# A recurrent layer in 2048 dependent steps: the output sum on GpSimd, y in two halves, and store addresses named earlier

## The reference, cut to what matters

```python
x = x + _L0_cond_ref(x, cond, W1, b1, W2, b2)   # per channel: x * (2 + gate), see below
x = x + _L1_cond_ref(cond, x, W_z, U_z, C_z, b_z, W_r, U_r, C_r, b_r, W, U, C, b)

def step(h, xs):                                # 2048 times, one after the other
    xzt, xrt, xht = xs
    z = sigmoid(xzt + h @ U_z + vz)
    r = sigmoid(xrt + h @ U_r + vr)
    hh = tanh(xht + r * h @ U + vh)
    h_new = (1.0 - z) * h + z * hh
    return (h_new, h_new)
```

## Time and profile before

| what | value |
|---|---|
| median of 3 runs | 6809.69 us (6809.19 to 6810.33) |
| the profiled execution, its own time | 6811.76 us |
| its span, first to last instruction | 6809.9 us |
| granted TensorE clock, mean | 0.996 |
| busy: PE, PEld, DVE, ACT, POOL | 88%, 83%, 73%, 49%, 0% |
| chain that ended last | PE 71%, DVE 26%, issue 3% |

### The profile page before, as it was taken

The page is one execution under the profiler, slowest core; times in us unless marked ns, Lnnn a source line. Parts: engine busy times, 40 slices in busy tenths (PEclk is TensorE's granted clock), DMA queues, the critical chain, the costliest instruction groups (busy, mean ns, idle before and its releaser), DMA issues.

```text
span 6809.9 us, 488240 instructions
## 1 busy us (share of the span) xinstructions
PE 5998.4 (88%) x200232; PEld 5642.2 (83%) x200232; DVE 4955.6 (73%) x43503; ACT 3331.6 (49%) x22603; POOL 3.5 (0%) x13
## 2 busy tenths in 40 slices
PE   7888888888888888888888888888888888888888
PEld 7888888888888888888888888888888888888888
DVE  5777777777777777777777777777777777777777
ACT  3444444444444444444444444444444444444444
POOL 0000000000000000000000000000000000000000
PEclk8999999999999999999999999999999999999999
DMA  2000000000000000000000000000000000000000
GB/s 84 17 18 15 18 17 18 17 17 17 18 17 18 15 18 17 18 18 15 18 17 18 17 18 15 18 17 18 17 17 17 18 17 18 15 18 18 17 18 15
DMA packets 80315, 129.97 MB, mean 19 GB/s; under 512 B 12336, under 2 KB 18480, under 8 KB 80304
## 3 DMA queue, kind: packets, MB, share of 16 engines
q1 hardware_dynamic: 80304, 129.81, 5.5%
HBM read 20.46 MB, written 8.65 MB: 4 GB/s over the span
## 4 chain that ended last, share of the span: by engine, by line
PE 71%; DVE 26%; issue 3%; SPq 0%; DMA 0%; ACT 0%; ACTq 0%; DVEq 0%
PE pair_r L252 30%; PE ps_z L252 24%; PE pair_h L252 17%; DVE pair_h L487 8%; DVE h_part L522 5%; DVE h_part L541 4%; DVE h_part L527 2%; DVE keep L523 2%; DVE zn L536 2%; DVE h_part L532 2%; PE ps_z L212 0%; DMA u_raw<-in_L_cond_U 0%; PE ps_o L212 0%; DVE u_max L424 0%; PE ps_x L224 0%
## 5 line engine op out<-in xcount | busy, mean ns | idle before, releaser
L252 PEld LDWEIGHTS pair_r<-h_part,u_part 128*128 128x128 f16 x65536 | 1845.1, 96 | 1119.9 <-DVE h_part L541 1115.8
L252 PE MATMUL pair_r<-h_part,u_part 128*128 128x32 f16 x65536 | 2048.7, 177 | 771.1 <-DVE h_part L541 758.6
L252 PE MATMUL pair_h<-rh_part,u_part 128*128 128x32 f16 x65536 | 2016.6, 177 | 12.5 <-DVE rh_part L505 12.5
L252 PE MATMUL ps_z<-h_part,u_part 128*128 128x32 f16 x65536 | 1961.5, 176 | 0.0
L252 PEld LDWEIGHTS pair_h<-rh_part,u_part 128*128 128x128 f16 x65536 | 1842.8, 96 | 17.3 <-DVE rh_part L505 15.7
L252 PEld LDWEIGHTS ps_z<-h_part,u_part 128*128 128x128 f16 x65536 | 1795.3, 95 | 0.0
L487 DVE TENSOR_REDUCE pair_r<-pair_r 128x4 f32<-128x20 f32 x4096 | 759.4, 186 | 818.1 <-PE pair_r L252 615.1
L351 ACT ACTIVATE pair_r<-pair_r 128x4 f32<-128x4 f32 x4096 | 644.8, 158 | 1445.1 <-DVE pair_r L487 1182.4
L487 DVE TENSOR_REDUCE pair_h<-pair_h 128x4 f32<-128x12 f32 x4096 | 717.7, 175 | 665.7 <-PE pair_h L252 665.7
L351 ACT ACTIVATE th_z<-ps_z 128x8 f32<-128x8 f32 x2048 | 364.1, 178 | 1046.0 <-DVE ps_z L487 1046.0
L337 ACT ACTIVATE pair_h<-xp 128x8 f32 (+1 forms) x2049 | 369.9, 181 | 807.8 <-DVE zn L536 807.8
(11 more groups left out here) (70 smaller groups left out, 3275.9 us busy)
## 6 DMA issues: line engine op xcount, KB each, us to landing
w_stage<-w_in SPq DMA_DIRECT2D x384, 256.0 KB, 2.3
x_tok<-in_x SPq DMA_DIRECT2D x68, 128.0 KB, 2.6
out_dram<-o_tok SPq DMA_DIRECT2D x66, 128.0 KB, 2.3
mlp_w<-in_L_cond_W SPq DMA_DIRECT2D x2, 1024.0 KB, 6.9
u_raw<-in_L_cond_U_r SPq DMA_DIRECT2D x1, 1024.0 KB, 5.6
u_raw<-in_L_cond_U_z SPq DMA_DIRECT2D x1, 1024.0 KB, 7.6
u_raw<-in_L_cond_U SPq DMA_DIRECT2D x1, 1024.0 KB, 10.3
w_in<-in_L_cond_W_r SPq DMA_DIRECT2D x4, 256.0 KB, 9.8
```

What stands on the lines that cost most here:

```text
L252: last = nc.tensor.matmul(bank[:, SLOT * m:SLOT * m + WIDE].rearrange("p (r n) -> p r n", n=n), u_part[:, g, part, k, gm * P:(gm + 1) * P] ...
```

## The change

Three edits.

1. `make_out` moves from VectorE to GpSimd. GpSimd gets a loop over the 32 blocks: it waits for s_z_th of the block's first step (the hist copy of the last token stands ahead of that tanh on ScalarE) and adds hist and y_cur with one `tensor_tensor`. It can't scale in the same instruction, so ScalarE's copy into hist is scaled by 1 / H_SCALE. The last output waits for s_copied on GpSimd.
2. `make_y` becomes two instructions of 128x256: the first behind step 2 of the turn, the second, which raises s_y_ok, behind step 3.
3. `store_projection` takes its semaphore count and two offsets, written as three `dve.snap` expressions behind step u = 0 of the round, and indexes flattened views of xp and v_bias with them, behind step u = 3 as before.

```diff
--- before.py
+++ after.py
@@ -185,6 +185,18 @@
             pool.wait_ge(s["umax_ok"], G)
             nc.gpsimd.partition_all_reduce(u_all[:, :], u_max[:, :], P, RMAX).then_inc(s["uall_ok"], 1)
 
+            def make_out(ring):
+                nc.gpsimd.tensor_tensor(oT[:, :, :], hist[:, bass.ds(ring, TB), :].rearrange("p t c -> p c t"),
+                                        y_cur[:, :, :], ALU.add).then_inc(s["o_sum"], 1)
+
+            with pool.Fori(0, NB) as n:
+
+
+                pool.wait_ge(s["z_th"], pool.snap(n * TB + 1))
+                make_out(pool.snap(((n + 1) % 2) * TB))
+            pool.wait_ge(s["copied"], 1)
+            make_out((NB - 1) % 2 * TB)
+
         @block.tensor
         def _(pe):
             pe.wait_ge(s["ident_ok"], 1)
@@ -360,7 +372,7 @@
                     for hf in range(2):
                         tanh(ps_r[hf][:, TANH:TANH + HS], ps_r[hf], R, HS, f"r{hf}_sum", t1, f"r{hf}_th")
 
-                    A(hist[:, prv, :], h_cur[:, :], ACT.Copy)
+                    A(hist[:, prv, :], h_cur[:, :], ACT.Copy, scale=1.0 / H_SCALE)
                     tanh(th_z[:, :], ps_z, Z, S, "z_sum", t1, "z_th")
 
                     seed(pair_r, R, nxt)
@@ -388,7 +400,7 @@
                 with act.Fori(0, GM) as i:
                     steps(act.snap(n * TB + i * BODY + TURN), BODY, act.snap((n % 2) * TB + i * BODY + TURN))
             act.wait_ge(s["h_ok"], T)
-            A(hist[:, (T - 1) % (2 * TB), :], h_cur[:, :], ACT.Copy).then_inc(s["copied"], 1)
+            A(hist[:, (T - 1) % (2 * TB), :], h_cur[:, :], ACT.Copy, scale=1.0 / H_SCALE).then_inc(s["copied"], 1)
             put_out(NB + 1)
 
         @block.vector
@@ -449,13 +461,16 @@
             mlp_layer(1)
             dve.wait_ge(s["gate_ok"], 1)
 
-            def make_y(nb):
-
-                dve.wait_ge(s["x_tr"], nb)
-                V.tensor_tensor(y_next[:, :, :], ps_x[:, :].rearrange("p (c t) -> p c t", t=TB),
-                                gate2[:, :].unsqueeze(2).broadcast_to([P, S, TB]), ALU.mult).then_inc(s["y_ok"], 1)
-
-            make_y(1)
+            def make_y(nb, part):
+                if part == 0:
+                    dve.wait_ge(s["x_tr"], nb)
+                made = V.tensor_tensor(y_next[:, half[part], :], ps_x[:, :].rearrange("p (c t) -> p c t", t=TB)[:, half[part], :],
+                                       gate2[:, half[part]].unsqueeze(2).broadcast_to([P, HS, TB]), ALU.mult)
+                if part == 1:
+                    made.then_inc(s["y_ok"], 1)
+
+            for part in range(2):
+                make_y(1, part)
             for g in range(G):
 
                 dve.wait_ge(s["uhi"], g + 1)
@@ -552,40 +567,35 @@
                 new_low(1)
                 V.tensor_tensor(h_cur[:, :], keep[:, :], zn[:, :], ALU.add).then_inc(s["h_ok"], 1)
 
-            def store_projection(count, i, ring):
+            def store_projection(count, at, bias):
 
                 dve.wait_ge(s["proj_mm"], count)
-                V.tensor_tensor(xp[:, i, bass.ds(ring, TB), :].rearrange("p t b -> p b t"),
+                V.tensor_tensor(xp.rearrange("p g t b -> p (g t b)")[:, bass.ds(at, TB * B)].rearrange("p (t b) -> p b t", b=B),
                                 ps_p[:, 0:P].rearrange("p (b t) -> p b t", t=TB),
-                                v_bias[:, i, :].unsqueeze(2).broadcast_to([P, B, TB]), ALU.add)
-
-            def make_out(ring):
-
-                V.scalar_tensor_tensor(oT[:, :, :], hist[:, bass.ds(ring, TB), :].rearrange("p t c -> p c t"), 1.0 / H_SCALE,
-                                       y_cur[:, :, :], ALU.mult, ALU.add).then_inc(s["o_sum"], 1)
+                                v_bias.rearrange("p g b -> p (g b)")[:, bass.ds(bias, B)].unsqueeze(2).broadcast_to([P, B, TB]), ALU.add)
 
             def steps(t0, count, proj=None, turn=None):
 
 
                 for u in range(count):
                     step(dve.snap(t0 + (u + 1)))
+                    if proj is not None and u == 0:
+                        n, i, ring = proj
+                        count, at, bias = dve.snap(n * GM + i + 2), dve.snap(i * (2 * TB * B) + ring * B), dve.snap(i * B)
                     if proj is not None and u == K - 1:
-                        store_projection(*proj)
-                    if turn is not None and u == 0:
-
-                        make_out(turn[0])
+                        store_projection(count, at, bias)
                     if turn is not None and u == 2:
-                        dve.wait_ge(s["y_copied"], turn[1])
-                        make_y(turn[2])
+                        dve.wait_ge(s["y_copied"], turn[0])
+                        make_y(turn[1], 0)
+                    if turn is not None and u == 3:
+                        make_y(turn[1], 1)
 
             with dve.Fori(0, NB) as n:
                 other = dve.snap(((n + 1) % 2) * TB)
-                steps(dve.snap(n * TB), TURN, turn=(other, dve.snap(n + 1), dve.snap(n + 2)))
+                steps(dve.snap(n * TB), TURN, turn=(dve.snap(n + 1), dve.snap(n + 2)))
                 with dve.Fori(0, GM) as i:
 
-                    steps(dve.snap(n * TB + i * BODY + TURN), BODY, proj=(dve.snap(n * GM + i + 2), i, other))
-            dve.wait_ge(s["copied"], 1)
-            make_out((NB - 1) % 2 * TB)
+                    steps(dve.snap(n * TB + i * BODY + TURN), BODY, proj=(n, i, other))
 
 
 # ---- launch: one core; inputs and outputs as the reference has them ----
```

## The result

| | before | after |
|---|---|---|
| median, 6 runs of each | 6809.89 us (6809.19 to 6812.67) | 6849.91 us (6849.31 to 6850.17) |
| ratio, 95% interval | | 1.0058 (1.0045 to 1.0071) |
| span of the profiled execution | 6809.9 us | 6847.6 us |
| granted TensorE clock, mean | 0.996 | 0.989 |

The change makes the kernel 0.58% slower, beyond the 0.2% that can be told from no change. The predicted time was 6847 us. The sum came out to within 3 us; its terms did not, as the rest shows.

The account below looks back on a forecast made before the run. TensorE and VectorE, passing the state back and forth, were taken to bound it. Terms -17.9 - 4.2 + 20.4 + 29.8 + 9.2 + 0.1 = +37.4 us gave 6847 us against the median; 8 in 10: 6806 to 6878.

Parts of the forecast that it names:

- the sum's leaving: VectorE, step with output sum L564: moving it off VectorE gives back 0.56 us in 32 blocks, 17.9 us.
- y in halves: VectorE behind h_cur: each 256-column half of y fits the 0.54 us gap, giving back 32 x 0.13 = 4.2 us.
- GpSimd's sum holds VectorE: Behind s_z_th: GpSimd's SBUF reads delay VectorE's two-SBUF-input instructions by 0.93 us a block, 29.8 us; ends 8 to 41.
- with a second input I take 1.2 us: Length of GpSimd's sum: four times the 0.28 us select is 1.14, taken as 1.2; bounds 0.52 and 1.55 us.
- the two that I named: VectorE's L527 and L541, both with two SBUF inputs, ahead of one of which a gap of some 0.9 us was expected.
- The reason that I gave for a disturbance: VectorE's SBUF path has no room: L564 with two SBUF inputs took 1.08 us, y with one PSUM source 0.68.
- The call: GpSimd's code-set call ahead of the sum: 11.4 us paid in block 0 only, stalling TensorE 9.2 us once.
- The store's registers: VectorE's three register instructions between h_cur and store grow from 339 to 392 ns, 53 ns exposed at 384 stores, 20.4 us.
- Like L564's (139): The store's second register instruction, losing a register sum and gaining a remainder and product, was taken at 139 ns.
- third rival: Store addresses get out of the way: 30.7 us gained in place of 20.4 lost, 6796 us; chance 8%.
- no disturbance: First rival: GpSimd and VectorE don't disturb each other, the 29.8 us go, +7.6, 6817 us; chance 24%.
- the call in each block: Second rival: every block pays the code call, TensorE waits 9.2 us each time, +292.8, 7102 us; chance 10%.

Follow-up runs that it names:

- edit 2 alone: Kernel before with only y made in two halves, in steps 2 and 3; 6803.1 us, executed once.
- the copy: Changed kernel with GpSimd only copying the strided hist rows (one SBUF input), y left out of the sum; 6827.0 us, executed once.
- the writing: Changed kernel with GpSimd's sum replaced by a one-element addition and three memsets, about as long as the sum; 6803.8 us, executed once.
- edit 3 alone: Kernel before with only the store's addresses given as flat offsets, the sum staying on VectorE; 6810.5 us, executed once.
- the call ahead of the loop: Changed kernel with one small GpSimd addition behind the all-reduce, ahead of the loop, to load the addition's code; 6847.8 us, executed once.
- weights first: As halves in the gap, but SyncE loads a block's first-round weights ahead of its wait for the evacuated output; 6810.2 us, 1.0003 of before.
- held addresses: Kernel before with edit 3 and the store's three values worked out at the round's head into held registers; 6795.4 us, 0.9982 of before.
- halves in the gap: Changed kernel with GpSimd's sum in two halves, released by s_hs1 ending steps 0 and 1, all consumers one step later; 6884.6 us, 1.0111 of before.
- halves at the same place: Changed kernel with GpSimd's sum in two halves, each behind z_th, one in step 0 and one in step 1; 6841.7 us, executed once.
- everything together: Sum halves in VectorE's gap, first weights loaded early, small addition ahead of the loop, y in step 3, store values in held registers; 6785.4 us, 0.9966 of before.
- edit 1 alone: Kernel before with only the output sum moved to GpSimd, y whole and the store as before; 6857.8 us, 1.0074 of before.

## Why the prediction was right, and which of its terms were not

**What bounds it, and the sum's leaving: right.** 32 x 0.56 = 17.9 us were to come back; with GpSimd's disturbance removed (it only writes) step 1 gives 17.5 in 31 blocks. y in halves: 4.2 forecast, 3.8 in 31 blocks, by the run of edit 2 alone from step 3.

**GpSimd's sum holds VectorE: the mechanism right, the size too low.** The term was 32 x 0.93 = 29.8; measured 40.3. The step that failed is the length: "with a second input I take 1.2 us", and it took 1.52, near the upper bound of 1.55 from three passes of a memset. With 1.52 in the prediction's own working the term would be 1.25 us a turn; measured 1.30. The sum also began 0.31 us behind the end of the tanh, not 0.41 (0.27 of these came from no row), and caught L538, which stands ahead of the two that I named. The reason that I gave for a disturbance, L564's 1.08 us against y's 0.68, compares two different instructions and no run took it up; what shows the hold is the copy and the writing. The copy then took 1.11: the select of the earlier trace rows, four times 1.14, was a good measure for one input, and the second added 0.4.

**The call: once, as forecast, and cheaper.** 9.2 us were entered from the 11.4 us gap of the earlier trace rows; block 0 lost 5.1 in all, its step 2 alone 5.4. The term was mis-sized by the gap that it took. From the call at 74.8 to the sum at 81.55 it is 6.7 us. The run that loads ahead of the loop shows 9.9 us for a switch in the start, so the gap that I took was real, but the switch in the loop is shorter. What makes the one longer than the other no run shows. Nor has the lower end of the 4 to 10 us that a stall was to take there a row behind it; TensorE waited 5.00 us.

**The store's registers: the right cause, half the price.** 53 ns were forecast (339 to 392), and it is 26 (107, 129 and 129 ns, 365 in sum), of which the fifth step shows 25: 9.2 us in 31 blocks for 20.4. "Like L564's (139)" was the step that failed, and the first instruction got cheaper (114 to 107). That edit 3 by itself moves nothing is confirmed. What the prediction took from the step's length, that the store alone makes the fifth step 0.08 us longer, was wrong by half: 40 ns are the store's; the 43 that stay are read off the rows as ScalarE's. The third rival would have gained at most 15 us, not 30.7.

**Not foreseen.** TensorE's clock: behind the stall it fell, 5.2 us in step 2 and, against the version without a stall, 1.3 in step 1, 6.5 in all. The last output cost 0.1, as entered. And 2.8 us were gained ahead of the first step. Those are chance. From the all-reduce to the first h_cur it is 48.7 to 48.8 us in four of the 14 traces (before, edit 3 alone, the call ahead of the loop, weights first) and 45.6 to 45.7 in the other ten, with the hold of step 0 taken off where there is one (the call ahead of the loop, the copy); held addresses, which touch nothing ahead of the first step, have the short start and edit 3 alone the long one. The executions of before itself lie between 6806.7 and 6813.3 us, and in the largest group 12 of 21 within 6806.7 to 6808.3 and nine within 6809.5 to 6811.9. In the traces it goes with the time at which TensorE's clock falls for the second time, 25.3 to 26.0 us behind the start of the all-reduce in the four and 26.1 to 27.9 in the ten; what sets that time stays open.

So +29.8 should have been +40.3, +20.4 was +9.2, +9.2 was +5.1, 0 was +6.5, and 2.8 came off by chance. The errors of the terms (+10.5, -11.2, -4.1, +6.5, -2.8, and some 1 in the rest) all but cancel, and that the total is so close is luck. Of the rivals, no disturbance fell with step 0 at 4.59 us, the call in each block with one stall in the whole trace, and the store with its start at 0.43 us behind h_cur (3243.48 to 3243.91 in the trace after).

## What to carry to other kernels

Work that is put on GpSimd isn't off VectorE's path if it reads SBUF: here it cost VectorE its own length less the time until VectorE's next instruction with two SBUF inputs would have ended (1.52 us cost 1.30), so place it where VectorE works from PSUM or is idle, and cut it to that gap (with the halves in the gap, two reductions of pair_r from PSUM took 0.49 us beside a half of the sum, as in the earlier trace rows without one). Before a step is made later, follow every queue that waits for it: the load of weights behind a harmless evacuation cost more (74.4 us) than the hold (40.3 us). And read the order of instructions before believing that a value is worked out where it is written; a value shared by two users became dearer for the second when the first left (26 ns at each store).

## What the hardware showed that I had not expected

- TensorE's granted clock fell from 1.00 to 0.50 behind stalls in which its next products waited 1.44 us (the change, 28 of 31 blocks) and 2.33 us (halves in the gap, 31 of 31), and stayed at 1.00 in 29 of 31 blocks behind one of 1.02 us (the copy) and in all 31 behind two of 0.78 and 0.71 us (halves at the same place). The length of one stall isn't the whole of it: with the weights first the granted clock fell to 0.50 in 8 of 31 blocks and with everything together in 6, in turns in which TensorE waited no longer than 0.63 us, and with edit 1 alone it fell twice. Four transposes of oT took 1.10 us at a granted clock of 0.50 (after) and 0.64 at 1.00 (before).
- The set of code that a kernel leaves on GpSimd seems to be found there by the next execution: in kernels that call the set of the addition on GpSimd (the change, the version that writes), the select of the identity follows its call after 0.24 us of idle time, at 1.17; where that set isn't called for (before, the copy), only after 11 us. It is so in all 14 traces: 1.17 to 1.43 us in eight, 12.1 to 12.7 in six. The time gained nothing from it, since the all-reduce waits for VectorE, and so for loads, until 29.96 us either way (29.74 before). The row of the timeline after:

```profile
1.17 0.29 POOL L176 TENSOR_SCALAR_AFFINE_SELECT ident<-ident 128x128 f32<-128x128 f32 x1 [0.24 <-POOL ident L174]
```

- The exposed part of a hold was the length of GpSimd's instruction less 0.21 to 0.23 us in three cases at this place (1.52, 1.11 and 0.85 us), so its price here can be read from that length alone.
- Left open: y's first half behind step 2 in the version with everything together, which should give back 7 us by the account, and ScalarE's remainder in the last step of a round, 43 ns x 384 = 16.5 us, weren't tried.
